# Alignment in a chained attention kernel: a boundary lag of two slots, scans seeded from PSUM, and the teacher rows loaded during the stage before

## The chip, the cores and the metric

One core of a Trainium2 chip runs the whole program in one launch. The metric is the device time of that launch in microseconds (us). A core has five engines that run on their own and meet at semaphores: TensorE (PE in the rows, its weight loads PEld), VectorE (DVE), ScalarE (ACT), GpSimd (POOL) and SyncE (SP), from whose queue most DMAs of this kernel are issued.

## The reference, cut to what matters

The program is a chain of four layers on `x` (8 batches of 256 rows of 256 numbers): cross attention, a mixture of experts that takes one expert a row, an alignment, a gated feed-forward, and further attention and expert layers. The change lies in the alignment and in the expert layer ahead of it. The alignment takes the teacher rows `ctx` (`small` below) and the layer-normalised rows of `x` (`large`) of each batch, finds the cheapest monotone path between them (dynamic time warping), and adds to each row of `x` the teacher rows that the path puts beside it.

```python
def _pairwise_euclidean(a, b):
    aa = jnp.sum(a * a, axis=-1)[:, None]
    bb = jnp.sum(b * b, axis=-1)[None, :]
    ab = a @ b.T
    return jnp.sqrt(jnp.maximum(aa + bb - 2.0 * ab, 0.0))

def _dtw_cost(D):          # R[i, j] = D[i, j] + min(R[i-1, j], R[i, j-1], R[i-1, j-1])
    ...

def _align_one(small, large):
    D = _pairwise_euclidean(small, large)
    R = _dtw_cost(D)
    i_idx, j_idx, valid = _backtrack(R, T_small, T_large)
    contrib = small[i_idx] * valid[:, None].astype(small.dtype)
    expanded = jnp.zeros((T_large, d), dtype=small.dtype).at[j_idx].add(contrib)
    return expanded
```

## The kernel before

`program` (L2775) runs the stages one after the other. Each is a function with its own tiles and semaphores in a `Scope`, closed by a barrier of all engines, and each lists the instructions of every engine by hand, in the order in which that engine takes them. All tensors are float32 where nothing else is said. `P` is 128, `NT` 16 is the number of row tiles, `QT` 2 the row tiles of a batch, `DC` 2 the halves of the 256 features.

**`moe` (L1821), called as `l0f` ahead of the alignment.** After the routing, 23 blocks (`NB`) of 128 gathered rows go through one expert each. GpSimd issues the indirect DMAs (expert weights `fetch`, rows `gather`, results `scatter`), and a block whose expert is that of the block two before fetches no weights. TensorE turns the rows (`turn`, L1895, read by VectorE in `read_t`, L2034, which counts `b_read`), multiplies up (L1911) and down (L1923); ScalarE applies Gelu in `gelu(j)` (L1950, L1957), eight activations a block; VectorE adds the bias. SP has four stores of the rows ahead of the blocks and nothing to issue during them; at the end it waits for all results (L1886) and loads them back. `keep_busy` (L79) issues matmuls on the identity whose result nobody reads.

**`alignment` (L2166), the stage that the change is about,** in four parts.

*Distances.* VectorE computes row statistics in `RowStats`: `moments` (L102) for the first 4 row tiles, then for the other 12, ScalarE takes the roots. GpSimd normalises two tiles a batch into `xn` (L2374), and fills the whole of `d` with 0 after the second batch (L2378) and the whole of `r` with a large number after the fourth (L2380). TensorE turns a batch (L2286), VectorE scales the turned rows by -2 (`minus_two`, L2462), ScalarE squares them (L2396), TensorE makes the products with the turned teacher rows `aT` (L2297) and the column sums of the squares (L2304). ScalarE also squares the teacher rows `ctx` with a sum for each (`aa`, L2420) and copies the column sums (L2403). VectorE adds the three terms into `d2` (`squared`, L2473), ScalarE cuts at zero and takes the root (L2407, L2409), and SP stores the batch to `dist` in DRAM (L2256). `d2` and its store semaphore `dd_out` have two buffers. SP first issues the loads of `aT` for batches 0 and 1, of `ctx` (2 MB), and of `aT` for 2 and 3 (256 KB each); `aT` for batches 4 to 7 follow as buffers come free. After the last store has landed SP loads `dist` back as `d` in a skewed layout (L2261, L2264): partition `8k + b` holds rows `16k` to `16k + 15` of batch `b`, moved right by `LAG * k` columns.

*Recurrence.* A slot `t` handles one column in each of the 16 row blocks (`KB`), block `k` at column `t - LAG * k`. There are `SLOTS = S + LAG * (KB - 1)` of them. VectorE takes the minimum of the two neighbours in the previous column (L2492) and then scans down the 16 rows (`tensor_tensor_scan`, L2497: `state = min(state, near) + d`). The scan starts from the last row of the block above, which another partition made `LAG` slots before: TensorE moves it by eight partitions with the matrix `shift` (L2317), ScalarE adds `outside` (a large number for the first block, 0 for the others) and writes it to `r[:, 0, 2 + t]` (L2430), from where the scan reads its start. Three semaphores carry this: `step` (a scan is done), `moved` (TensorE), `passed` (ScalarE).

```python
for t in range(LAG, SLOTS):                                    # TensorE
    pe.wait_ge(step, t - LAG + 1)
    if t >= LAG + 2:
        pe.wait_ge(passed, t - LAG - 1)
    nc.tensor.matmul(psS[t % 2][:, 0:1], consts["shift"][:], r[:, WB, 2 + t - LAG:3 + t - LAG],
                     start=True, stop=True).then_inc(moved, 1)
```

At slots that are a multiple of `LAG` VectorE also waits for the load of one further block of `d` (`d_first`), and at slot 128 for the right halves (`d_second`).

*Backtrack.* VectorE works through tiles of `CH` x `SLOTS` half-precision elements: comparisons (L2515 to L2518), one long scan (L2519), fifteen rounds of two short operations and a scan (L2523 to L2525), a difference (L2528), fifteen picks of the entries (L2534) and sixteen inside the blocks (L2542). Meanwhile TensorE and ScalarE make keys and values for a later layer (L2330, L2336, L2436 to L2443).

*Spread.* The found spans become 0/1 matrices, and TensorE multiplies them with `ctx` (L2361); VectorE adds to `x`.

## Time and profile before

| | |
|---|---|
| three runs | 2449.93, 2453.03 and 2457.38 us, median 2453.03 |
| the profiled execution | 2449.72 us, its span 2447.9 us |
| granted TensorE clock, mean over the span | 0.828 of full |
| busy share of the span: PE, DVE, ACT, POOL | 81%, 65%, 48%, 39% |

"Busy" is the time in which an engine executes, as a share of the span from the first to the last instruction. The stages follow one another, so a share is an average over stretches that have different limits. All instants below are us from the start of the span. "x16" is the number of instructions in a row; "[3.08 <-DVE ...]" says that the engine sat idle for 3.08 us and which work ended that; SPq and POOLq are the issuing of DMAs. A fp32 matmul stands as two instructions.

### The profile page before, as it was taken

The page shows a single profiled execution, that of the slowest core. Times are in us where ns is not written, and L with a number is a line of the kernel's source. Part 1 is how long each engine was busy: PE and PEld are TensorE (multiplying, and loading weights), DVE is VectorE, ACT ScalarE, POOL GpSimd, SP SyncE. Part 2 cuts the span into 40 slices and gives each one's busy share as a digit, 9 for nine tenths or more (in the row PEclk, how much of TensorE's full clock was granted, in tenths as well). Part 3 has the DMA queues.
Part 4 walks back from the last instruction along what each step waited for, and adds up shares of the span by engine and source line. Part 5 has one row for each costly group of instructions (what it writes and reads, how often), then busy time and mean ns, then how long its engine had stood idle before and what let it go on. Part 6 is the DMA issues. An engine that isn't in the chain of part 4 may idle for free. (4 is left out here: it accounts for less than half of the span.)

```text
span 2447.9 us, 40733 instructions
## 1 busy us (share of the span) xinstructions
PE 1983.4 (81%) x13451; PEld 1615.2 (66%) x13451; DVE 1596.9 (65%) x5265; ACT 1182.9 (48%) x3292; POOL 952.3 (39%) x918
## 2 busy tenths in 40 slices
PE   7985999599948967977999937777777877775788
PEld 5663898499937855655999925566665656654555
DVE  6775111588973247853111168999999999993786
ACT  3544232455321115543232325787777787773354
POOL 3311454300007023303555525666666666661210
PEclk9997999755779989987999975586777778767899
DMA  3112565520314012305364330010000000002442
GB/s 96 62 49 90 195 242 176 150 35 1 120 38 178 0 65 75 104 32 193 128 214 148 103 121 25 1 40 10 31 31 18 31 10 22 31 10 83 154 155 77
DMA packets 102085, 204.56 MB, mean 84 GB/s; under 512 B 20318, under 2 KB 70774, under 8 KB 93942
## 3 DMA queue, kind: packets, MB, share of 16 engines
q1 hardware_dynamic: 77752, 116.23, 14.3%
q0 software_dynamic: 23808, 85.50, 10.2%
q8 instruction: 109, 1.79, 0.3%
q14 instruction: 96, 0.79, 0.1%
q10 hardware_dynamic: 320, 0.26, 0.0%
HBM read 216.31 MB, written 55.35 MB: 111 GB/s over the span
## 5 line engine op out<-in xcount | busy, mean ns | idle before, releaser
L814 DVE MATCH_REPLACE8 l3a_left<-l3a_top,l3a_left 128x256 f32<-128x256 f32 x768 | 309.2, 411 | 0.0
L807 DVE MAX8 l3a_top<-l3a_left 128x8 f32<-128x256 f32 x768 | 286.4, 415 | 0.0
L514 POOL TENSOR_TENSOR l3a_prob<-l3a_expd,l3a_rest 128x512 f32<-128x512 f32 x128 | 162.7, 1271 | 210.3 <-ACT l3a_rest L596 209.4
L369 PEld LDWEIGHTS l3a_psO<-l3a_probT,l3a_vp 128*128 128x128 f32 x1024 | 182.3, 264 | 69.1 <-ACT l3a_probT L612 39.5
L369 PE MATMUL l3a_psO<-l3a_probT,l3a_vp 128*128 128x128 f32 x1024 | 206.3, 365 | 24.1 <-ACT l3a_probT L612 24.1
L351 PE MATMUL l3a_psT<-all_ident,l3a_prob 128*128 128x128 f32 x512 | 111.6, 358 | 108.9 <-POOL l3a_prob L514 108.3
L501 POOL TENSOR_TENSOR l3a_kept<-l3a_raw_sc,l3a_mone 128x512 f32<-128x512 f32 x128 | 163.5, 1277 | 69.4 <-ACT l3a_raw_sc L580 65.8
L1957 ACT ACTIVATE l2f_hT<-l2f_psH,l2f_wt 128x128 f32<-128x128 f32 x312 | 89.2, 369 | 209.5 <-PE l2f_psH L1911 209.5
L507 POOL TENSOR_TENSOR l3a_sc_sb<-l3a_kept,l3a_mlow 128x512 f32<-128x512 f32 x128 | 165.4, 1292 | 10.0
L351 PEld LDWEIGHTS l3a_psT<-all_ident,l3a_prob 128*128 128x128 f32 x512 | 79.6, 184 | 125.7 <-POOL l3a_prob L514 125.4
L2317 PE MATMUL dtw_psS<-dtw_r,all_shift 128*128 128x1 f32 x596 | 152.7, 356 | 10.2 <-DVE dtw_r L2497 9.8
L2317 PEld LDWEIGHTS dtw_psS<-dtw_r,all_shift 128*128 128x128 f32 x596 | 149.2, 311 | 14.0 <-DVE dtw_r L2497 10.8
L1911 PEld LDWEIGHTS l2f_psH<-l2f_xsT,l2f_wt 128*128 128x128 f32 x1248 | 145.3, 192 | 3.4 <-DVE l2f_xsT L2038 1.5
L1911 PE MATMUL l2f_psH<-l2f_xsT,l2f_wt 128*128 128x128 f32 x1248 | 145.8, 275 | 1.0 <-DVE l2f_xsT L2038 1.0
L596 ACT ACTIVATE l3a_rest<-l3a_left,l3a_nmax 128x256 f32<-128x256 f32 x256 | 116.0, 503 | 62.2 <-DVE l3a_left L814 61.8
L1923 PE MATMUL l2f_psY<-l2f_wt,l2f_hT 128*128 128x256 f32 x624 | 141.0, 379 | 0.0
L1923 PEld LDWEIGHTS l2f_psY<-l2f_wt,l2f_hT 128*128 128x128 f32 x624 | 115.6, 190 | 14.2
L2627 POOL TENSOR_TENSOR l1f_kx<-l1f_kx,l1f_cosT 128x512 f32<-128x512 f32 x8 | 11.0, 1374 | 280.2 <-DMA l1f_kx<-k_at 280.2
L589 ACT ACTIVATE l3a_expd<-l3a_sc_sb,l3a_nmax 128x256 f32<-128x256 f32 x256 | 116.3, 501 | 4.1
L1988 POOL DMA_INDIRECT l2f_wt<-in_L_table,l2f_widx x78 | 79.9, 1024 | 97.4 <-ACT l2f_hT L1957 49.3
L2430 ACT ACTIVATE dtw_r<-dtw_psS,all_outside 128x1 f32<-128x1 f32 x298 | 77.9, 261 | 81.4 <-PE dtw_psS L2317 81.4
L1957 ACT ACTIVATE l0f_hT<-l0f_psH,l0f_wt 128x128 f32<-128x128 f32 x184 | 52.7, 368 | 128.8 <-PE l0f_psH L1911 128.8
(571 smaller groups left out, 4725.8 us busy)
## 6 DMA issues: line engine op xcount, KB each, us to landing
key_at<-l3a_a_k SPq DMA_DIRECT2D x8, 768.0 KB, 3.3
kv_at<-dtw_vd SPq DMA_DIRECT2D x8, 512.0 KB, 2.9
k_at<-dtw_kx SPq DMA_DIRECT2D x8, 512.0 KB, 4.3
l1f_kx<-k_at SPq DMA_DIRECT2D x8, 512.0 KB, 4.4
kv_at<-l1f_k SPq DMA_DIRECT2D x8, 512.0 KB, 3.1
l2a_k<-kv_at SPq DMA_DIRECT2D x8, 512.0 KB, 5.7
l2a_vd<-kv_at SPq DMA_DIRECT2D x8, 512.0 KB, 6.7
l2f_yb<-rows_y SPq DMA_DIRECT2D x8, 512.0 KB
```

The costliest lines, as they stand in the source:

```text
L351: mm = nc.tensor.transpose(psT[u % 2][:, kc, e, :], prob[:, u % 4, e, kc * P:kc * P + P], ident[:])
L369: mm = nc.tensor.matmul(psO[y % 2][:, c, 0:P], vp[:, p, kc, c, g * P:g * P + P], probT[:, u % 2, kc, e, :], start=(j == 0 and e == 0 and k ...
L501: nc.gpsimd.tensor_tensor(kept[:], raw_sc[:, u % 2, :, :], mone[:, p, qt, :].unsqueeze(1).to_broadcast([P, 2, S]), ALU.mult)\
L507: nc.gpsimd.tensor_tensor(sc_sb[:, u % 4, :, :], kept[:], mlow[:, p, qt, :].unsqueeze(1).to_broadcast([P, 2, S]), ALU.add)\
L514: nc.gpsimd.tensor_tensor(prob[:, u % 4, :, :], expd[:, u % 2, :, :], rest[:, u % 2, :, :], ALU.subtract).then_inc(picked, 1)
L589: last = nc.scalar.activation(expd[:, u % 2, e, :], sc_sb[:, u % 4, e, :], ACT.Exp, bias=nmax[:, u % 2, e:e + 1])
L807: ins = nc.vector.max(top[:, e, eight], rows[:, e, :] if r else scores[:, e, :])
L814: ins = nc.vector.match_replace(out=rows[:, e, :], in_to_replace=top[:, e, eight], in_values=rows[:, e, :] if r else scores[:, e, :], imm_ ...
L1911: mm = nc.tensor.matmul(psH[2 * p + f // 4][:, f % 4, :], w1[p][c_][f], xsT[:, p, c_, :], start=(c_ == 0), stop=(c_ == DC - 1))
L1923: mm = nc.tensor.matmul(psY[p][:, 0:D], hT[:, p, f, :], w2[p][f], start=(f == 0), stop=(f == FC - 1))
L1957: nc.scalar.activation(hT[:, p, f, :], psH[2 * p + f // 4][:, f % 4, :], ACT.Gelu, bias=wt1[:, p, ROW_B1 + f:ROW_B1 + f + 1]).then_inc(g_d ...
L2317: nc.tensor.matmul(psS[t % 2][:, 0:1], consts["shift"][:], r[:, WB, 2 + t - LAG:3 + t - LAG], start=True, stop=True).then_inc(moved, 1)
```

## The change

- The statistics of the alignment are taken in three groups, of 4, 4 and 8 tiles. VectorE scales batches 0 and 1 before the third.
- A new class `Teacher` holds `ctx_sb`, `aT`, `aa` and their semaphores over both stages. `moe` gets it as `early` (in its first call only): SP loads `ctx` and the first four `aT` after the second transposed read (`b_read` at 2), and ScalarE squares the teacher rows of one batch after the activations of each of blocks 8 to 15.
- `d2` and `dd_out` have four buffers.
- `LAG` is 2, so `SLOTS` is 286 instead of 301, and tiles and passes of that width shrink.
- Two matmuls fill the columns of two PSUM tiles with `outside`. The shift of slot `t` adds to column `t` of one of them. The scan takes its start from that column and covers one row more: row 0, with `near` large and `d` zero, so that it writes its start into `r[:, 0]` itself. ScalarE's step and `passed` go.
- GpSimd fills only the borders of `d`, `near` and `r`, ahead of the normalising.
- TensorE begins the stage with `keep_busy(..., 2)`.

```diff
@@ RowStats
-    def __init__(self, s, nc, x, rstd, mean, negative=False):
+    def __init__(self, s, nc, x, rstd, mean, negative=False, cuts=(FIRST, NT)):
...
     def tiles(self, g):
-        return ((0, self.FIRST), (self.FIRST, NT))[g]
+        return self.cuts[g], self.cuts[g + 1]
@@ moe, sync
+            if early:
+                sp.wait_ge(b_read, 2)
+                early.load(sp)
             for p in range(2):
                 sp.wait_ge(rows_out[p].sem, rows_out[p].base + 16 * ((NB + 1 - p) // 2))
@@ moe, scalar
             for j in range(NB):
                 gelu(j)
+                if early and early.FROM <= j < early.FROM + B:
+                    early.squares(act, j - early.FROM)
@@
+class Teacher:
+    FROM = 8
...
+    def load(self, sp):
+        sp.dma_start(self.ctx_sb[:], self.ctx.rearrange("b (t p) d -> p (b t) d", p=P)).then_inc(self.ctx_in, 16)
+        for b in range(4):
+            self.load_turned(sp, b)
+
+    def squares(self, act, b):
+        if b == 0:
+            act.wait_ge(self.ctx_in, 16)
+        for n in range(b * QT, b * QT + QT):
+            if n >= 2:
+                act.wait_ge(self.aa_done, n - 1)
+            self.nc.scalar.activation(self.junk[:, n % 2, :], self.ctx_sb[:, n, :], ACT.Square,
+                                      accum_out=self.aa[:, n:n + 1]).then_inc(self.aa_done, 1)
@@
-LAG = 3
+LAG = 2
 SLOTS = S + LAG * (KB - 1)
@@ alignment
-        stats = RowStats(s, nc, x, rstd, nmean, negative=True)
+        stats = RowStats(s, nc, x, rstd, nmean, negative=True, cuts=(4, 8, NT))
...
-        d2 = s.sb("d2", [P, 2, QT, S])
-        junk = s.sb("junk", [P, 2, D])
-        d = s.sb("d", [P, WB, SLOTS])
-        near = s.sb("near", [P, 2, WB])
+        d2 = s.sb("d2", [P, 4, QT, S])
+        d = s.sb("d", [P, 1 + WB, SLOTS])
+        near = s.sb("near", [P, 2, 1 + WB])
@@ alignment, sync
-            load(0)
-            load(1)
-            sp.dma_start(ctx_sb[:], ctx.rearrange("b (t p) d -> p (b t) d", p=P)).then_inc(ctx_in, 16)
-            load(2)
-            load(3)
             sp.dma_start(down_at[:], consts["down_at"]).then_inc(tab_in, 16)
             for b in range(B):
                 if b >= 1 and b + 3 < B:
-                    load(b + 3)
+                    sp.wait_ge(d_ps, b)
+                    teacher.load_turned(sp, b + 3)
                 sp.wait_ge(dd_done, b + 1)
@@ alignment, tensor
+            keep_busy(nc, psS[0][:], ident, 2)
             turn(0)
...
                 distances(b)
+            for p in range(2):
+                nc.tensor.matmul(psS[p][:, 0:SLOTS], ident[:], consts["outside"][:].to_broadcast([P, SLOTS]), start=True, stop=False,
+                                 skip_group_check=True)
             for t in range(LAG, SLOTS):
                 pe.wait_ge(step, t - LAG + 1)
-                if t >= LAG + 2:
-                    pe.wait_ge(passed, t - LAG - 1)
-                nc.tensor.matmul(psS[t % 2][:, 0:1], consts["shift"][:], r[:, WB, 2 + t - LAG:3 + t - LAG],
-                                 start=True, stop=True).then_inc(moved, 1)
-            pe.wait_ge(passed, SLOTS - LAG)
+                nc.tensor.matmul(psS[t % 2][:, t:t + 1], consts["shift"][:], r[:, WB, 2 + t - LAG:3 + t - LAG], start=False,
+                                 stop=(t >= SLOTS - 2), skip_group_check=True).then_inc(moved, 1)
@@ alignment, gpsimd
+            nc.gpsimd.memset(d[:, 0:1, :], 0.0)
+            for a, z in ((0, LAG * (KB - 1)), (S, SLOTS)):
+                nc.gpsimd.memset(d[:, 1:, a:z], 0.0).then_inc(pad_set, 1)
+            nc.gpsimd.memset(near[:], BIG).then_inc(corner, 1)
+            nc.gpsimd.memset(r[:, :, 1:2], BIG).then_inc(corner, 1)
+            nc.gpsimd.memset(r[:, 0:1, 2:2 + LAG], BIG).then_inc(corner, 1)
             for b in range(B):
...
-                if b == 1:
-                    nc.gpsimd.memset(d[:], 0.0).then_inc(pad_set, 1)
-                if b == 3:
-                    nc.gpsimd.memset(r[:], BIG).then_inc(corner, 1)
@@ alignment, scalar
-            stats.roots(act)
+            stats.root(act, 0)
+            stats.root(act, 1)
+            act.wait_ge(teacher.aa_done, NT)
             squares(0)
-            act.wait_ge(ctx_in, 16)
+            stats.root(act, 2)
...
-            act.wait_ge(corner, 2)
-            for t in range(LAG, SLOTS):
-                act.wait_ge(moved, t - LAG + 1)
-                nc.scalar.activation(r[:, 0, 2 + t:3 + t], psS[t % 2][:, 0:1], ACT.Identity,
-                                     bias=consts["outside"][:, 0:1], scale=1.0).then_inc(passed, 1)
@@ alignment, vector
                 dve.wait_ge(d_ps, b + 1)
                 dve.wait_ge(b_read, b + 1)
-                dve.wait_ge(aa_done, QT * (b + 1))
-                if b >= 2:
-                    dve.wait_ge(dd_out[b % 2], 16 * (b // 2))
+                if b >= 4:
+                    dve.wait_ge(dd_out[b % 4], 16 * (b // 4))
...
             stats.moments(dve, 0)
             stats.moments(dve, 1)
             minus_two(0)
+            minus_two(1)
+            stats.moments(dve, 2)
             for b in range(B):
-                if b + 1 < B:
+                if 2 <= b + 1 < B:
                     minus_two(b + 1)
                 squared(b)
...
-                nc.vector.tensor_tensor(near[:, t % 2, :], r[:, 1:1 + WB, 1 + t], r[:, 0:WB, 1 + t], ALU.min)\
+                nc.vector.tensor_tensor(near[:, t % 2, 1:], r[:, 1:1 + WB, 1 + t], r[:, 0:WB, 1 + t], ALU.min)\
                     .then_inc(near_set, 1)
                 dve.wait_ge(near_set, t + 1)
                 if t >= LAG:
-                    dve.wait_ge(passed, t - LAG + 1)
-                nc.vector.tensor_tensor_scan(r[:, 1:1 + WB, 2 + t], near[:, t % 2, :], d[:, :, t], r[:, 0, 2 + t:3 + t],
+                    dve.wait_ge(moved, t - LAG + 1)
+                    above_first = psS[t % 2][:, t:t + 1]
+                else:
+                    above_first = r[:, 0, 2 + t:3 + t]
+                nc.vector.tensor_tensor_scan(r[:, 0:1 + WB, 2 + t], near[:, t % 2, :], d[:, :, t], above_first,
                                              ALU.min, ALU.add).then_inc(step, 1)
```

## Rows read from the trace of the kernel before

**Rows 1.** Timeline of the start of the alignment: start us, us busy, instruction, [idle before]
```profile
437.42 0.89 SPq L2243 DMA_DIRECT2D dtw_aT<-in_ctxT  x2
...
439.97 2.17 POOL L2374 TENSOR_SCALAR dtw_xn<-all_x,dtw_nmean,all_rstd 128x256 f32<-128x256 f32 x4 [15.14 <-DVE all_rstd L115]
...
445.23 1.22 DVE L2462 TENSOR_SCALAR dtw_xm<-dtw_psT 128x512 f32<-128x512 f32 x2
...
446.40 3.38 PE L2297 MATMUL dtw_psD<-dtw_xm,dtw_aT 128*128 128x256 f32 x8 [3.08 <-DVE dtw_xm L2462]
...
448.49 0.42 ACT L2420 ACTIVATE dtw_junk<-dtw_ctx 128x256 f32<-128x256 f32 x1 [1.53 <-DMA dtw_ctx<-in_ctx]
```

**Rows 2.** Timeline: distance matmuls of two later batches
```profile
453.95 1.89 PE L2297 MATMUL dtw_psD<-dtw_xm,dtw_aT 128*128 128x256 f32 x8
...
456.98 1.89 PE L2297 MATMUL dtw_psD<-dtw_xm,dtw_aT 128*128 128x256 f32 x8
```

**Rows 3.** A wait (total, times, longest); windows: engines' busy us, PEclk, DMA share, GB/s
```profile
PEld l0f_psY L1923 <- DMA l0f_wt<-in_L_table,l0f_widx: 0.2, 1, 0.2
...
259.00:271.00 12.00, 11.48 (x88) 10.83 (x88) 1.72 (x5) 4.57 (x16) 5.13 (x6) 1.00 0.08 23
...
437.00:449.00 12.00, 4.79 (x14) 3.61 (x15) 8.64 (x39) 3.20 (x8) 8.89 (x10) 0.50 0.86 266
```

**Rows 4.** Timeline of the last batch of distances
```profile
470.97 1.03 PE L2304 MATMUL dtw_psB<-dtw_xsq,all_ones 128*128 128x256 f32 x4
...
473.76 0.88 DVE L2473 SCALAR_TENSOR_TENSOR dtw_d<-dtw_psD,dtw_aa,dtw_bb 128x256 f32<-128x256 f32 x2 [2.14 <-DMA dist<-dtw_d]
...
475.33 0.63 ACT L2409 ACTIVATE dtw_d<-dtw_d 128x512 f32<-128x512 f32 x1
```

**Rows 5.** The recurrence's two lines: ns min/median/max, first and last start us
```profile
L2497 DVE TENSOR_TENSOR_SCAN dtw_r<-dtw_near,dtw_r,dtw_d x301: 251/252/255, 481.5 to 635.5; 128x16 f32<-128x16 f32 x151
...
  ACT dtw_r L2430: 0.7, 3
...
L2492 DVE TENSOR_TENSOR dtw_near<-dtw_r x301: 183/185/189, 481.2 to 635.3; 128x16 f32<-128x16 f32 x151
```

**Rows 6.** Backtrack by lines: busy us, mean ns of one; idle before
```profile
L2525 DVE TENSOR_TENSOR_SCAN dtw_v<-dtw_left,dtw_via 128x301 f16<-128x301 f16 x15 | 11.8, 785 | 0.5
L2519 DVE TENSOR_TENSOR_SCAN dtw_uz<-dtw_left,dtw_uz 128x4832 f16<-128x4832 f16 x1 | 10.2, 10225 | 0.0
...
L2515 DVE TENSOR_TENSOR dtw_dg<-dtw_r 128x4816 f16<-128x4816 f32 x1 | 5.2, 5174 | 0.0
...
L2528 DVE TENSOR_TENSOR dtw_du<-dtw_uz 128x4816 f16<-128x4816 f16 x1 | 2.7, 2673 | 0.0
```

**Rows 7.** Small VectorE operations elsewhere, ns min/median/max
```profile
L2080 DVE TENSOR_TENSOR_SCAN l0f_incl<-l0f_ones,l0f_tot x8: 176/178/191, 232.0 to 232.7; 128x16 f32<-128x16 f32 x8
...
L2549 DVE TENSOR_SCALAR dtw_ends<-dtw_psB x1: 175/175/175, 710.1 to 710.1; 128x16 f32<-128x16 f32 x1
```

**Rows 8.** Timeline of single slots of the recurrence
```profile
482.48 0.25 DVE L2497 TENSOR_TENSOR_SCAN dtw_r<-dtw_near,dtw_r,dtw_d 128x16 f32<-128x16 f32 x1
482.84 0.18 DVE L2492 TENSOR_TENSOR dtw_near<-dtw_r 128x16 f32<-128x16 f32 x1
...
621.81 0.25 DVE L2497 TENSOR_TENSOR_SCAN dtw_r<-dtw_near,dtw_r,dtw_d 128x16 f32<-128x16 f32 x1 [0.24 <-ACT dtw_r L2430]
...
622.12 12.69 PEld L2317 LDWEIGHTS dtw_psS<-dtw_r,all_shift 128*128 128x128 f32 x50 [0.22 <-DVE dtw_r L2497]
...
622.74 0.26 ACT L2430 ACTIVATE dtw_r<-dtw_psS,all_outside 128x1 f32<-128x1 f32 x1 [0.46 <-PE dtw_psS L2317]
```

**Rows 9.** Timeline of the expert stage
```profile
242.69 6.25 PE L83 MATMUL l0f_psX<-all_ident 128*128 128x512 f32 x8
...
259.48 0.42 DVE L2038 COPY l0f_xsT<-l0f_psX 128x256 f32<-128x256 f32 x1 [6.62 <-PE l0f_psX L1900]
...
371.04 1.14 ACT L1957 ACTIVATE l0f_hT<-l0f_psH,l0f_wt 128x128 f32<-128x128 f32 x4 [4.38 <-PE l0f_psH L1911]
```

More of the change, by code:

```diff
@@ L126, in roots @@
     def roots(self, act):
-        for g in range(2):
+        for g in range(len(self.cuts) - 1):
             self.root(act, g)
@@ L2211, in alignment @@
         du = s.sb("du", [P, CH, SLOTS], F16)
-        above_min, side, on = d, (xn, xsq), xm2
+        above_min, side, on = d[:, 1:, :], (xn, xsq), xm2
         psT = [s.ps(f"psT{i}", [P, 512]) for i in range(2)]
@@ L2218, in alignment @@
         ends_ps = psE[:, 0:2 * QT * B].rearrange("p (k q b) -> p k q b", k=2, q=QT)
-        ctx_in, tab_in = s.sem("ctx_in"), s.sem("tab_in")
-        a_in, dd_out = [s.sem(f"a_in{p}") for p in range(4)], [s.sem(f"dd_out{p}") for p in range(2)]
+        tab_in = s.sem("tab_in")
+        a_in, dd_out = teacher.a_in, [s.sem(f"dd_out{p}") for p in range(4)]
         d_first, d_second = [s.sem(f"d_first{k}") for k in range(KB)], s.sem("d_second")
-        x_norm, t_done, m2_done, sq_done, b_ps, b_read, d_ps, d2_done, cut, dd_done, aa_done = (
+        x_norm, t_done, m2_done, sq_done, b_ps, b_read, d_ps, d2_done, cut, dd_done = (
             s.sem(n) for n in ("x_norm", "t_done", "m2_done", "sq_done", "b_ps", "b_read", "d_ps",
-                               "d2_done", "cut", "dd_done", "aa_done"))
-        corner, pad_set, near_set, step, moved, passed = (
-            s.sem(n) for n in ("corner", "pad_set", "near_set", "step", "moved", "passed"))
+                               "d2_done", "cut", "dd_done"))
+        corner, pad_set, near_set, step, moved = (
+            s.sem(n) for n in ("corner", "pad_set", "near_set", "step", "moved"))
         col_set = s.sem("col_set")
```

69 lines of the change are left out of this document (34 added, 35 removed).

## The prediction, made before the changed kernel ran

> **What bounds the kernel now.** I read the page first: its chain that ended last spreads over many stages and names nothing of the alignment, so the change is priced where its code runs, from 437.42 us on in the timeline, and in the expert stage ahead of it. Four stretches matter.
>
> The prologue, 437.4 to 481.2 us, makes the distances [rows 1]. TensorE waits 3.08 us for VectorE, which scales the first tile only at 445.23, after the statistics of all 16 row tiles. The first distance matmuls take 3.38 us, such eight take 1.89 us later [rows 2]: the granted clock is 0.50 (the 1.2 GHz level) to 449 us [rows 3]. From there TensorE goes on with one batch each 3.03 us. At the end VectorE waits 2.14 us for a `dist` store to free one of two buffers [rows 4].
>
> The recurrence, 481.5 to 635.8 us, is VectorE's own two-step chain [rows 5]: 301 slots, each a minimum (185 ns) and a scan (252 ns) with hand-overs of some 35 ns, 0.51 us together. TensorE and ScalarE carry a boundary value for a scan three slots on; it was late only three times, 0.7 us in all. The backtrack, 635.8 to 710 us, is again VectorE back to back [rows 6], with kv work under it. The expert stage is TensorE's: it idled 0.2 us for weights [rows 3].
>
> **Slots.** LAG 2 for 3 makes 256 + 2x15 = 286 slots of 301. From the first scan's start to the last's are 635.5 - 481.5 = 154.0 us over 300 steps, 0.5135 us each, the 16 slots with a further wait for a block of `d` included (their number stays). Fifteen fewer save 7.7 us. The scan gets a 17th element: (785 - 178)/(301 - 16) = 2.1 ns by the scans of 301 and of 16 elements [rows 6, 7], 0.6 us in all. **Saved: 7.1 us** at an unchanged slot.
>
> **Is the shorter lag met?** By the timeline of one slot [rows 8]: the scan starts at 621.81, the shift's weight load at 622.12, ScalarE's read of its result at 622.74. So the result is there 0.93 us after the scan began. The new wait for it stands as a second wait ahead of the next-but-one scan. Where a slot had such a further wait (scan from 482.48 for 0.25 us, next minimum at 482.84), the next instruction started 0.11 us after the scan's end instead of 0.04: 0.07 us more. Together 1.00 us against two slots, 1.02 us. It just fits, since ScalarE's 0.26 us drop out. Behind the wait on VectorE's queue stand that scan and the next minimum, for which TensorE alone is waiting. Bounds: no cost, or a chain 0.06 us longer, half of it per slot: 0.03 x 286 = 8.6 us. I take 0, since each term was seen.
>
> **What a seed in PSUM costs the scan.** No row has a PSUM scalar. The scan of 16 elements from a constant takes 178 ns, this one, from a column in SBUF, 252 ns [rows 5, 7]: the column costs at most 74 ns. Bounds: -74 ns (a PSUM column is free; but then TensorE's chain of 1.00 us holds the slot at 0.50, so in effect -0.01 us a slot, 2.9 us) and +74 ns (it costs twice, 286 x 0.074 = 21.2 us). A tensor read from PSUM is no dearer: 175 ns for a 16-element operation against 185 ns from SBUF [rows 5, 7]. I take 0, by that nearest row.
>
> The Trainium skill, VectorE: DVE Perf Modes, section on the TRN2 errata, charges a VectorE instruction 120 cycles when it reads PSUM and 58 for SBUF; the 62 cycles would be an estimated 65 ns a slot, and the sum would by it end 3.5 us above the time of before. The rows do not show that gap for a tensor input, and no run here shows it for a scalar.
>
> **Prologue.** VectorE's second statistics group shrinks from 12 tiles to 4. Four tiles took from 437.42 to 439.97, with the start; 12 took from there to 445.23 [rows 1]. Four more end near 442.2, where the first scaling now starts. The third group (8 tiles, some 3.9 us between those two) then runs to 447.3 under TensorE's first batch. First distance matmul: 442.9 for 446.40, **3.5 us**. `keep_busy(2)` is four instructions; eight took 6.25 us ahead of the expert blocks [rows 9], so 3.1 us, 437.5 to 440.6, before the first normalised tiles are there at 441.1 (439.97 and half of 2.17): free. It may lift the clock for the first batch, by 0 to 3.38 - 1.89 = 1.5 us; I take 0.7. The first four `aT` tiles are long there and load 4 to 7 come ahead of need by a us or so; nothing counted. Against that ScalarE's third root waits for VectorE until 447 and holds the first copy of the column norms: 0.5 us lost.
> At the end, from the last column sums (472.0) to the last root (475.96) are 3.96 us. With four buffers it is a copy of some 0.4, add 0.88, cut and root 0.63 each and hand-overs, 2.7 us: **1.3 us** [rows 4]. The 5.3 us from root to first minimum stay: store, then first block load; SP has nothing new ahead of them. The seed matmuls come after the last batch, in that time. Sum 3.5 + 0.7 - 0.5 + 1.3 = **5.0 us**, range 3 to 7. Squares of `ctx` leave ScalarE (two of 0.42 us a batch and two accumulator reads, some 1.2 us [rows 1]), under TensorE's 3.03 us, so that counts for nothing. GpSimd's two big fills become six small ones, ahead of 439.97 when it is first needed; uncovered they would cost 1 us once.
>
> **Backtrack.** 286 columns for 301, at each row's slope [rows 6]: three passes of 5.17, one scan of 10.22 and two passes of 2.67 us lose 5% of all but their fixed part, 1.5 us; fifteen rounds lose 32 ns in the scan and 8 ns in each of two operations, 0.7 us; sixteen picks lose 16 ns each, 0.3 us. **2.5 us**, all on VectorE's chain.
>
> **The expert stage**, where things are added. Five loads (3 MB) are issued after the second transposed read, which ends at 259.9 us [rows 9]. From 259 to 271 the queues move 23 GB/s, against 266 from 437 to 449 in the old place [rows 3]. There these loads took from 437.42 to 448.49, 11.1 us [rows 1], so they are in by 271. Cost 0; if the cover is gone, TensorE waits for weights, at the very most those 11.1 us, more likely 2. ScalarE gets those 1.2 us of squares behind the activations of blocks 8 to 15, where it sits idle 4.38 us [rows 9]. Cost 0, and 9.6 us for eight blocks without that cover.
>
> **Sum.** 7.1 + 5.0 + 2.5 = 14.6 us off the profiled execution's own 2449.72 us (span 2447.9 and 1.8 around it): 2435.1 us. The median of the three runs shown is 3.3 us above that execution, so 2438.4 us on its scale. What a measurement of this kernel can tell from no change is 0.3%, 7.4 us.
>
> **Rivals.**
> *TensorE's chain sets the slot.* For it: the margin is 0.02 us. Against: it is made of seen parts, and a longer scan gives it room. A slot of 0.53 us costs 0.02 x 286 = 5.7 us: 2444.1. Chance 0.14.
> *The PSUM seed makes the scan slower*, which ends on the other side. It acts in 286 slots on the engine that bounds them and decides from 14.6/286 = 51 ns on. For it: a column from SBUF already costs up to 74 ns. Against: the tensor reads. At +74 ns: 2438.4 + 21.2 = 2459.6. Chance 0.14.
> *The prologue gives nothing*: the clock and the moved statistics only shift the wait, or the loads meet the weights. 2443.4. Chance 0.10.
> *The half-precision passes lose their double rate.* Rows of 302 elements all began alike, rows of 287 alternate. The two passes would go from 2.67 to about 5 us and thirty short operations gain 0.15 us each: 9.2 us, 2447.6. Against: inputs that begin one element in, and an output in rows of 301, go at that rate now [rows 6]. Chance 0.02. The Trainium skill, same page, Mode 2x_1P, wants 4-byte alignment; by that rule this is what comes, and the trace of before already disagrees.
> *Forecast*: 0.60.
>
> **Numbers.** 2438.4, given as 2438. Below, all bounds at their best (2.0 in the prologue, 2.9 for the slot) and the scatter of some 3 us: 2431. Above, TensorE's chain and the failed prologue together, or three quarters of the PSUM case: 2454. Faster by over 0.3%: the forecast and most of the first and third rival, 0.76. Within 0.3%: the rest of these and a PSUM cost of 25 to 77 ns, 0.17. Slower: more than that, or two mishaps, 0.07.
>
> **What would show it.** The scan's row at 252 to 256 ns if the seed is free, 310 or more if not; scan starts 0.51 us apart, and no waits of the scan for `dtw_psS`. First distance matmul near 442.9 us, first minimum near 476. Passes of 4576 elements near 4.92 and 2.55 us. In the expert stage no wait for `l0f_wt`. A scan or a slot 50 ns longer would make the forecast wrong.

## The result and the profile after

| | before | after |
|---|---|---|
| median of 7 runs each, us | 2454.80 (2449.93 to 2457.38) | 2445.49 (2435.65 to 2451.26) |
| the profiled execution, span, us | 2449.72, 2447.9 | 2445.64, 2443.8 |
| granted TensorE clock, mean | 0.828 | 0.825 |
| busy share: PE, DVE, ACT, POOL | 81%, 65%, 48%, 39% | 81%, 65%, 45%, 39% |

The ratio is 0.996, with an interval of 0.9945 to 0.9975: 0.4% faster, 9.3 us by the medians where 14.6 were forecast. The time lies inside the range given, 7 us above the point.

The whole program is a poor place to read such a change. The alignment alone went from 293.16 to 280.54 us, 12.6 us less, and the stage behind the next three (`l3a`) started 15.1 us earlier (1420.8 for 1435.9), but that execution's two last stages took 10 us longer. So the steps are read from the alignment. All instants with a "+" below are us after the first instruction of an engine that writes a tile of the alignment (437.51 before, 438.17 after).

The start of the alignment after the change, from its timeline (columns as in [rows 1]):

```profile
438.21 3.75 PE L83 MATMUL dtw_psS<-all_ident 128*128 128x512 f32 x4 [14.34 <-PEq L61]
...
440.71 2.17 POOL L2407 TENSOR_SCALAR dtw_xn<-all_x,dtw_nmean,all_rstd 128x256 f32<-128x256 f32 x4 [1.17 <-DVE all_rstd L115]
...
443.02 1.37 DVE L2482 TENSOR_SCALAR dtw_xm<-dtw_psT 128x512 f32<-128x512 f32 x2 [0.17 <-PE dtw_psT L2312]
...
443.86 1.97 PE L2323 MATMUL dtw_psD<-dtw_xm,teacher_aT 128*128 128x256 f32 x8 [0.19 <-DVE dtw_xm L2482]
...
448.83 0.30 PEld L2330 LDWEIGHTS dtw_psB<-dtw_xsq,all_ones 128*128 128x128 f32 x2 [0.38 <-ACT dtw_xsq L2425]
```

The stage starts 0.7 us later than before, so the first distance matmul, at 443.86, stands at +5.68 for +8.90 before [rows 1]. The wait for VectorE is 0.19 us for 3.08, the eight matmuls take 1.97 us for 3.38. The last row is the price of the third statistics group, whose root holds up ScalarE's square: 0.38 us. GpSimd's six small fills are covered: it waits 1.17 us for VectorE before it can normalise. The windows of both stretches (busy us per engine, then granted clock, DMA share, GB/s) answer [rows 3]:

```profile
259.00:271.00 12.00, 11.48 (x86) 10.51 (x85) 1.72 (x5) 4.28 (x16) 4.89 (x5) 1.00 0.84 259
438.00:443.00 5.00, 4.79 (x9) 1.96 (x9) 4.17 (x21) 2.08 (x4) 3.54 (x10) 0.50 0.08 16
443.00:446.30 3.30, 3.11 (x15) 2.62 (x16) 3.28 (x9) 0.60 (x1) 2.17 (x4) 0.98 0.00 0
```

The teacher's loads now fill the queues from 259 us on, where 23 GB/s went before, and TensorE is as busy there as before, 11.48 us of 12. The clock is at its upper level (2.4 GHz) from the first distance matmul on, after 4.8 us of filling and transposes at the lower.

The recurrence and the end of the backtrack's passes, by lines and shapes (busy us, mean ns of one, idle before), answer [rows 5, 6]:

```profile
L2521 DVE TENSOR_TENSOR_SCAN dtw_r<-dtw_near,dtw_psS,dtw_d 128x17 f32<-128x17 f32 x284 | 73.6, 259 | 11.2 <-DVE dtw_near L2513 1.4
L2513 DVE TENSOR_TENSOR dtw_near<-dtw_r 128x16 f32<-128x16 f32 x286 | 54.4, 190 | 17.9 <-DMA dtw_d<-dist 6.8
...
L2521 DVE TENSOR_TENSOR_SCAN dtw_r<-dtw_near,dtw_r,dtw_d 128x17 f32<-128x17 f32 x2 | 0.5, 254 | 0.1
```
```profile
L2549 DVE TENSOR_TENSOR_SCAN dtw_v<-dtw_left,dtw_via 128x286 f16<-128x286 f16 x15 | 11.3, 754 | 0.5
L2543 DVE TENSOR_TENSOR_SCAN dtw_uz<-dtw_left,dtw_uz 128x4592 f16<-128x4592 f16 x1 | 9.7, 9724 | 0.0
...
L2552 DVE TENSOR_TENSOR dtw_du<-dtw_uz 128x4576 f16<-128x4576 f16 x1 | 2.5, 2550 | 0.0
```

The scan takes 259 ns with its start in PSUM and 254 in the first two slots, whose start lies in SBUF; it was 252 with 16 elements. The minimum, whose text was hardly touched, takes 190 for 185. VectorE's waits in the loop name no `dtw_psS`: TensorE's value is always there. The passes are shorter in proportion to 286 of 301 columns, the half-precision ones too.

### The profile page after: what moved, and what is told of

It reads as the page before. It is cut to its first block and busy times, and to the rows that moved or that the text cites. A ratio compares the mean times of both kernels' runs of the same rounds, so it can differ in the third digit from the quotient of the medians.

```text
span 2443.8 us, 40081 instructions
## 1 busy us (share of the span) xinstructions
PE 1991.6 (81%) x13431; PEld 1616.9 (66%) x13431; DVE 1595.4 (65%) x5237; ACT 1105.0 (45%) x2995; POOL 944.3 (39%) x922
## 3 DMA queue, kind: packets, MB, share of 16 engines
q1 hardware_dynamic: 77752, 116.22, 14.5%
## 5 line engine op out<-in xcount | busy, mean ns | idle before, releaser
L2345 PEld LDWEIGHTS dtw_psS<-dtw_r,all_shift 128*128 128x128 f32 x568 | 142.2, 311 | 15.8 <-DVE dtw_r L2521 9.6
L341 PE MATMUL l3a_sc<-l3a_kT,l3a_q 32*128 32x256 f32 x512 | 105.0, 530 | 2.0 <-ACT l3a_q L550 2.0
```

The source lines that it names most:

```text
L2345: nc.tensor.matmul(psS[t % 2][:, t:t + 1], consts["shift"][:], r[:, WB, 2 + t - LAG:3 + t - LAG], start=False, stop=(t >= SLOTS - 2), skip ...
```

## The experiments

This table sets the parts of the alignment side by side, each from one profiled execution (us; the middle columns from the stage's start; "loop" is from the first minimum to the last scan's end). The alignment ends here 0.73 us behind its last instruction, in every row; the expectation of `again` counts to that instruction, 279.8 us for the 280.54 of the table.

| kernel | first distance matmul | last root ends | first minimum | slots, loop | rest | alignment |
|---|---|---|---|---|---|---|
| before | 8.90 | 38.46 | 43.74 | 301, 154.52 | 94.90 | 293.16 |
| after | 5.68 | 32.59 | 37.99 | 286, 150.85 | 91.70 | 280.54 |
| again | 5.41 | 32.31 | 37.69 | 286, 151.07 | 91.34 | 280.09 |
| lag3 | 5.41 | 32.31 | 37.81 | 301, 156.93 | 94.32 | 289.06 |
| old_lag2 | 8.70 | 37.88 | 43.14 | 286, 185.69 | 92.10 | 320.93 |
| wide_r | 5.68 | 32.56 | 38.01 | 286, 150.04 | 91.97 | 280.02 |
| no_early | 5.68 | 37.99 | 43.33 | 286, 150.28 | 90.85 | 284.47 |
| late_sq | 5.67 | 38.82 | 44.10 | 286, 150.43 | 92.14 | 286.66 |
| old_cuts | 8.56 | 37.22 | 42.63 | 286, 150.18 | 91.14 | 283.94 |
| no_busy | 5.67 | 32.99 | 38.28 | 286, 150.89 | 92.57 | 281.74 |
| two_d2 | 5.68 | 33.72 | 38.95 | 286, 150.93 | 91.39 | 281.26 |
| seed_sbuf | 5.68 | 33.05 | 38.35 | 286, 149.56 | 92.17 | 280.08 |
| near_psum | 5.67 | 32.72 | 38.07 | 286, 152.04 | 91.06 | 281.18 |
| best | 5.64 | 32.22 | 37.64 | 286, 154.95 | 91.18 | 283.77 |

Seven of the kernels (`after`, `again`, `lag3`, `wide_r`, `seed_sbuf`, `near_psum`, `best`) have the same prologue: their last root spans 0.8 us and their first minimum 0.7, though up to the fifth batch they agree within 0.3. "Rest" is all but the same code in every row with 286 slots except `old_lag2`, and spans 1.7 us. So the parts are read column by column, where 1 us can be told and 0.3 us cannot, and the sum in the last column is the coarser figure.

### again: the changed kernel once more

No edit. 

> The changed kernel once more, nothing edited. Its alignment stage took 279.8 us in the first profile, 12.6 us less than before, but the two attention stages at the end took 816.2 and 187.8 us against 809.8 and 183.8. Theory A (the late stages' times move from execution to execution, whatever the alignment does): the alignment within 0.5 us of 279.8, the late stages off by several us from 816.2 and 187.8 in either direction. Theory B (the change costs the late stages something): they come out within 1 us of 816.2 and 187.8. The time: about 9 us below before, 0.994 to 0.998.

Measured: 2443.92 us (2435.91 to 2450.84, 7 runs), ratio 0.9948 [0.9927, 0.9969]. The alignment took 280.09 us, the last two stages 806.7 and 188.7 us, where the first profile had 816.2 and 187.8 and the kernel before 809.8 and 183.8. That is theory A: the alignment repeats to half a microsecond and `l3a` alone moves by 10 us between executions of the same code. The 10 us that the last stages seemed to give back were that scatter, and the 12.6 us stand. They would be a ratio of 0.995, which lies inside both intervals. The medians of the whole say 9.3 us in the first comparison and 14.5 in this one (2443.92 against 2458.38 for the kernel before).

### lag3 and old_lag2: what makes a slot

`lag3` puts the three-slot lag back, with seeds in three PSUM tiles; `old_lag2` puts the two-slot lag into the kernel before.

```diff
-LAG = 2
+LAG = 3
+            seeds = [psS[0], psS[1], psB[0]]
-                nc.tensor.matmul(psS[t % 2][:, t:t + 1], ...
+                nc.tensor.matmul(seeds[t % 3][:, t:t + 1], ...
```

> The changed kernel with LAG 3 again: 301 slots, seeds in three PSUM tiles instead of two (the third is one of the column-sum tiles), all else kept. Theory A (a slot's length is VectorE's own two operations; the PE chain has room at LAG 2): scan starts stay 0.52 us apart at the median, the recurrence is 15 slots = 7.9 us longer and the backtrack 2.5 to 3 us, so 10 to 11 us are lost against the changed kernel, and the time is about that of before (ratio 0.998 to 1.002). Theory B (TensorE's chain holds the slot at 0.52): with three slots of room it falls to 0.508 to 0.513, and only 6 to 8 us are lost.

> The kernel before with LAG 2 alone, ScalarE still carrying the boundary. The chain from a scan's start to the seed in SBUF is 0.93 us to ScalarE's start and 0.26 us for its operation, and 0.04 to 0.11 us to the next scan: 1.23 to 1.30 us over two slots. Theory A (the shorter lag needs the seed from PSUM): 0.62 to 0.65 us a slot, recurrence 177 to 186 us for 154, so the kernel loses 20 to 29 us against before in that stretch less 2.5 to 3 in the backtrack: 2468 to 2480 us. Theory B (the lag was free anyway, the seed from PSUM unneeded): slot 0.51, 146 us, the kernel 10 us faster than before.

Measured: `lag3` 2452.99 us (10 runs), ratio 0.9975 [0.9953, 0.9998], alignment 9.0 us longer than `again`. `old_lag2` 2480.11 us (one run), its loop 185.69 us. The lines of the recurrence, first of `lag3`, then of `old_lag2`:

```profile
L2517 DVE TENSOR_TENSOR dtw_near<-dtw_r 128x16 f32<-128x16 f32 x286 | 53.5, 187 | 11.0
L2525 DVE TENSOR_TENSOR_SCAN dtw_r<-dtw_near,dtw_psS,dtw_d 128x17 f32<-128x17 f32 x190 | 49.2, 259 | 7.0 <-DVE dtw_near L2517 0.3
```
```profile
L2497 DVE TENSOR_TENSOR_SCAN dtw_r<-dtw_near,dtw_r,dtw_d 128x16 f32<-128x16 f32 x270 | 68.2, 253 | 45.3 <-ACT dtw_r L2430 35.2 <-DVE dtw_near L2492 0.4
L2492 DVE TENSOR_TENSOR dtw_near<-dtw_r 128x16 f32<-128x16 f32 x271 | 51.4, 190 | 17.2 <-DMA dtw_d<-dist 6.6
```

The scan is 259 ns at either lag, so the shorter lag costs the scan nothing; a slot of `lag3` is 516 ns at the median against 520, and the 4 ns are the minimum's. So TensorE's chain does not hold the slot at a lag of two, theory A in the mechanism. The loss is smaller than A said, the loop 5.9 to 6.1 us longer for 7.9: fifteen slots are 7.7 us, the faster minimum gives back some 1.2 and fewer of the unexplained gaps (last section) some 0.8. The seed in PSUM and the lag belong together: with ScalarE still in the chain VectorE waits 35.2 us for it, and a slot has a mean of 650 ns, theory A's 0.62 to 0.65 us. The seed alone, at the old lag, loses: loop 156.93 for 154.52 us.

### wide_r: the minimum's 5 ns

The minimum took 185 to 187 ns in the two kernels whose rows of `r` lie 303 elements apart, and 190 in those at 288, at either lag. This kernel is the changed one with rows 303 apart.

```diff
-        r = s.sb("r", [P, 1 + WB, 2 + SLOTS])
+        r = s.sb("r", [P, 1 + WB, 17 + SLOTS])
```

> The changed kernel with the rows of r 303 elements apart as before, instead of 288. In the changed kernel the minimum takes 191 ns for 185 and the scan with a PSUM seed 259 ns for 252. Theory A (the distance of r's rows costs it): the minimum is back at 185 ns, the slot at 0.514, 1.5 us saved in 286 slots. Theory B (the minimum's output, which now begins one element in, costs it, or its 17-element neighbour): the minimum stays at 190 or 191 ns, and nothing is saved. The scan: 259 ns by both if its 5 ns are the PSUM seed's.

```profile
L2521 DVE TENSOR_TENSOR_SCAN dtw_r<-dtw_near,dtw_psS,dtw_d 128x17 f32<-128x17 f32 x283 | 73.3, 259 | 11.3 <-DVE dtw_near L2513 1.4
L2513 DVE TENSOR_TENSOR dtw_near<-dtw_r 128x16 f32<-128x16 f32 x284 | 53.1, 187 | 11.1
```

The minimum is back at 186 ns (median), the scan stays at 259, the slot's median is 517, and the loop 0.8 to 1.0 us shorter. The row distance is the cause; only these two distances were tried, and why 288 is dearer than 303 no run here tells. In time: 2443.28 us (10 runs), ratio 0.9937 [0.9918, 0.9955], not told apart from `again`.

### seed_sbuf and near_psum: the price of PSUM

`seed_sbuf` leaves the boundary values between the row blocks out of the recurrence; `near_psum` computes the same as the changed kernel.

```diff
-                    above_first = psS[t % 2][:, t:t + 1]
+                    above_first = consts["outside"][:, 0:1]
```
```diff
+            nearp = psT[0][:, 0:2 * (1 + WB)].rearrange("p (k j) -> p k j", k=2)
-                nc.vector.tensor_tensor(near[:, t % 2, 1:], ...
+                nc.vector.tensor_tensor(nearp[:, t % 2, 1:], ...
-                nc.vector.tensor_tensor_scan(r[:, 0:1 + WB, 2 + t], near[:, t % 2, :], ...
+                nc.vector.tensor_tensor_scan(r[:, 0:1 + WB, 2 + t], nearp[:, t % 2, :], ...
```

> The scan takes its first value from a constant column in SBUF instead of the column in PSUM; the shift matmul, its wait and everything else stay. So the boundary values between the sixteen column blocks are left out of the recurrence. Theory A (reading the scalar from PSUM costs the scan 5 ns and nothing else): scan 254 ns for 259, slot median 515 for 520 ns, loop 1.4 us shorter, 149.5 us. Theory B (the 5 ns belong to the second wait or to the 17th column, not to where the scalar lies): scan stays at 259 ns, slot 520. Theory C (PSUM also delays the next instruction's start, which the scan's own duration does not show): slot 510 or less with the scan at 254.

> The minimum of each slot is written to PSUM and the scan reads its 17 elements from there, on top of the seed; the rest is the changed kernel (and TensorE's kv work waits for the last slot). It doubles the suspected cost of PSUM in a slot and puts it on the tensor operand and on a write. Theory A (PSUM costs a few ns an access at this size, as with the seed): scan 259 to 270 ns, minimum 191 to 200 ns, slot median 520 to 540. Theory B (a fixed price of some 60 ns falls on each access of PSUM, and the seed escaped it as a scalar): scan or minimum 50 to 70 ns longer, slot 575 or more, the loop 16 to 35 us longer.

The recurrence by lines, first of `seed_sbuf`, then of `near_psum`:

```profile
L2521 DVE TENSOR_TENSOR_SCAN dtw_r<-dtw_near,all_outside,dtw_d 128x17 f32<-128x17 f32 x272 | 69.2, 255 | 10.5 <-DVE dtw_near L2513 1.0
L2513 DVE TENSOR_TENSOR dtw_near<-dtw_r 128x16 f32<-128x16 f32 x275 | 52.4, 190 | 17.3 <-DMA dtw_d<-dist 6.7
```
```profile
L2524 DVE TENSOR_TENSOR_SCAN dtw_r<-dtw_psT,dtw_psS,dtw_d 128x17 f32<-128x17 f32 x273 | 70.3, 258 | 10.2 <-DVE dtw_psT L2516 0.6
L2516 DVE TENSOR_TENSOR dtw_psT<-dtw_r 128x16 f32<-128x16 f32 x273 | 54.0, 198 | 10.6
```

With the scalar in SBUF the scan is 254 ns and the slot's median 515 for 520: theory A, 5 ns a slot and nothing hidden behind it, 1.4 us in all. With 17 elements more read from PSUM the scan is not longer at all (258 for 259), and the minimum, which now writes there, takes 7 ns more; the slot's median is 526, theory A again. Both times of the whole (2444.43 and 2448.20 us, one run each) say nothing beyond that.

The Trainium skill, VectorE: DVE Perf Modes, section on the TRN2 errata, whose 62 cycles came to an estimated 65 ns, is contradicted for this kernel: the seed read from PSUM costs 5 ns and a tensor read none. The Trainium skill's 4-byte rule, same page, Mode 2x_1P, is contradicted by the row of `dtw_du` above, 2550 ns for 4576 elements out of rows 287 long, 0.56 ns each where the passes that read float32 took 1.07 before [rows 6].

### no_early, late_sq and old_cuts: what moved the prologue

`no_early` takes the teacher's loads and squares back into the alignment; `late_sq` is that with the squares one place later on ScalarE; `old_cuts` is the changed kernel with statistics of 4 and 12 tiles.

```diff
@@ no_early: moe gets no teacher; alignment, sync and scalar
+            teacher.load_turned(sp, 0)
+            teacher.load_turned(sp, 1)
+            sp.dma_start(ctx_sb[:], ...).then_inc(teacher.ctx_in, 16)
...
-            act.wait_ge(teacher.aa_done, NT)
+                    teacher.squares(act, b)
                     row_norms(b)
@@ late_sq: behind squares(b + 1)
-                    teacher.squares(act, b)
                     row_norms(b)
                 if b + 1 < B:
                     squares(b + 1)
+                if b < B:
+                    teacher.squares(act, b)
@@ old_cuts
-        stats = RowStats(..., negative=True, cuts=(4, 8, NT))
+        stats = RowStats(..., negative=True, cuts=(4, NT))
```

> The teacher's rows and their squares go back into the alignment: five loads issued at its start, two squares per batch on ScalarE between the column norms, VectorE's sum waiting for them; all the rest is the changed kernel. In the changed kernel the first distance matmul starts 5.68 us after the alignment's start, and the last root ends at +32.6 us. Theory A (my prediction's: the moved loads gave nothing, because the first block of aT is there long before it is used and ScalarE's squares lie under TensorE's batch): first distance matmul and last root within 0.5 us of that, alignment 280 to 281 us; the expert stage's last activations end 1 us or less earlier. Theory B: the first block of aT would land only at some +7 us (before, it was wanted only at +8.9), so that the earlier statistics are worth nothing without the earlier loads: first distance matmul at +7 or later, alignment 1.5 to 4 us longer. Theory C: ScalarE's squares between the roots lengthen each batch: first matmul unchanged, last root 1 us or more later.

> The statistics go back to two groups, of 4 and 12 tiles; the loads stay early, the clock is still kept up, the rest is the changed kernel. The first distance matmul then starts after all 16 tiles' statistics: before, that was at +8.9 us with the first scaling at +7.8; now +5.68. Theory A (the third group is what moved the start): first distance matmul at +8.4 to +9.0, alignment 2.5 to 3.3 us longer, 283 us. Theory B (the late third group costs later what the early start gains: ScalarE's root of it sits ahead of the first column norms and VectorE's scaling of later tiles waits): the end of the last root moves by less than 1.5 us, alignment 281 to 282 us.

> As the run with the teacher's rows loaded and squared inside the alignment, but each batch's two squares stand on ScalarE behind the squares of the next batch's transposed tile instead of ahead of the column norms. That run had its first distance matmul at +5.68, its third at +15.24 (changed kernel: +12.06), and its last root at +38.0 us (+32.6), with TensorE waiting 3.5 us for the squared tile, which stood behind ScalarE's wait for the teacher's rows (landed at +12.1). Theory A (it is the place on ScalarE's queue that cost, not the ScalarE time nor the load's): TensorE's wait goes, the third batch's matmuls start at +13 to +14 (held now only by VectorE's sum, which needs the row norms at +13), last root at +34 to +36. Theory B (ScalarE's extra 1.2 us per batch is what cost): last root at +37 or later.

Measured, one run each: 2453.34, 2443.70 and 2453.81 us; the alignment 3.9 to 4.4, 3.4 to 3.9 and 6.1 to 6.6 us longer than in the two runs of the changed kernel. In `no_early` the first distance matmul starts at +5.68 as expected by A (its `aT` is there), and yet the last root ends 5.4 us later. Its timeline:

```profile
454.30 0.42 ACT L2193 ACTIVATE teacher_junk<-teacher_ctx 128x256 f32<-128x256 f32 x1 [2.25 <-DMA teacher_ctx<-in_ctx]
...
455.38 0.58 ACT L2430 ACTIVATE dtw_xsq<-dtw_psT 128x512 f32<-128x512 f32 x1
...
456.01 1.13 PE L2335 MATMUL dtw_psB<-dtw_xsq,all_ones 128*128 128x256 f32 x4 [3.14 <-ACT dtw_xsq L2430]
...
457.44 3.56 PE L2328 MATMUL dtw_psD<-dtw_xm,teacher_aT 128*128 128x256 f32 x8
```

ScalarE stands at the first teacher square until `ctx` has landed, at +12.1, and behind it stands the square that TensorE needs: TensorE waits 3.14 us, and the clock it had is gone, so the third batch's eight matmuls take 3.56 us instead of 1.89:

```profile
447.80:452.00 4.20, 4.12 (x21) 3.68 (x22) 4.05 (x18) 0.85 (x2) 1.56 (x3) 1.00 1.08 358
456.00:461.10 5.10, 5.08 (x18) 4.22 (x19) 2.51 (x6) 3.58 (x12) 1.09 (x2) 0.67 0.18 56
```

The granted clock is 1.00 before the wait and 0.67 after it. Together 3.14 and 1.67 us are 4.8 of the 5.4. That number is theory C's, but its cause is not: from the start of the fourth batch's distance matmuls to the eighth's it is 12.4 us for 12.0 in the changed kernel, and the difference is a wait of 0.44 us for the sixth batch's `aT`. So the squares themselves lengthen no later batch. In the kernel before the same load of `ctx` was in at +10.98 [rows 1], and TensorE's late start covered it. `late_sq` was to take only the queue's part away, and A of its text failed: TensorE's second batch is no longer held and the third starts at +14.15 for +15.24, but the squares now hold VectorE's sum, and VectorE's next scaling, which TensorE needs, stands behind that. VectorE waited for the squares in all eight batches, 16.8 us, and TensorE stood just the same:

```profile
455.73 2.65 PE L2328 MATMUL dtw_psD<-dtw_xm,teacher_aT 128*128 128x256 f32 x8 [1.89 <-DVE dtw_xm L2488]
...
458.18 1.91 PE L2335 MATMUL dtw_psB<-dtw_xsq,all_ones 128*128 128x256 f32 x4
```

So it is the late landing of `ctx` that costs, and the place on the queue chooses who waits. The last root at +38.8 is theory B's number, but B's cause, ScalarE's added 1.2 us a batch, cost nothing a batch in `no_early`. In `late_sq` the new place costs more later on: its last root comes 6.4 us behind the start of the last batch's matmuls, for 5.5 in the changed kernel.

`old_cuts` starts its first distance matmul at +8.56 and is never caught up: first minimum 4.6 to 4.9 us later than in the changed kernel. Theory A has the cause and the start right (+8.4 to +9.0) and the loss too small: behind that start the first eight matmuls take 3.44 us for 1.97, and the sixth batch waits 0.55 us for its `aT`. The two parts are one. Against the kernel before, the early loads without the new cuts gain 1.1 us (42.63 for 43.74, about the buffers' share below), the new cuts without the early loads 0.4 us (43.33), both 5.75 to 6.05; all three figures have the four buffers in them.

### no_busy and two_d2

`no_busy` leaves out the `keep_busy` at the start; `two_d2` goes back to two distance buffers.

```diff
@@ no_busy
-            keep_busy(nc, psS[0][:], ident, 2)
@@ two_d2 (and every index % 4 of d2 and dd_out to % 2)
-        d2 = s.sb("d2", [P, 4, QT, S])
+        d2 = s.sb("d2", [P, 2, QT, S])
```

> The four filling matmuls ahead of the alignment's first transposes are left out. In the changed kernel the granted clock is 0.98 in the first batch and its eight distance matmuls take 1.97 us; before, at 0.50, they took 3.38. Theory A (the filling alone keeps the clock up; worth the 1.4 us measured in the matmuls and up to 1 us more in transposes and column sums): granted clock 0.50 for the first batch, eight matmuls 3.0 to 3.5 us, the last root 1.5 to 2.5 us later, alignment 282 us. Theory B (the clock is up because the work now comes sooner, without the filling): clock near 1, no difference. Theory C: the clock falls, but the first batch waits for other engines anyway: matmuls 3.4 us, alignment within 0.7 us.

> Two distance buffers in place of four; the rest is the changed kernel. Before, VectorE waited 2.14 us for a store in the last batch. Theory A (the prediction's 1.3 us): the wait comes back in the last batches only, the last root ends 1.0 to 2.2 us later, alignment 281.1 to 282.5 us. Theory B (with an earlier start, all batches run sooner than the stores return, so that every batch waits): 3 us or more longer. Theory C (the four buffers gave nothing, the stores are in time): within 0.5 us.

Measured, one run each: 2450.54 and 2446.11 us. Without the filling the first eight distance matmuls take 2.63 us for 1.97, and the fifth batch's start at +18.53, for +18.04 to +18.27 in the seven kernels with the same prologue: 0.3 to 0.5 us. The last root, 0.4 to 0.7 us later than in the changed kernel's two runs, is inside those kernels' own spread. That is theory C's size in the prologue, with less of a fall in the clock than C named; the rest of the alignment's 1.2 to 1.7 us stands in the column that scatters. From `old_cuts` comes the condition of its use:

```profile
446.94 3.44 PE L2323 MATMUL dtw_psD<-dtw_xm,teacher_aT 128*128 128x256 f32 x8 [3.15 <-DVE dtw_xm L2481]
```

There the filling ran just as long, then TensorE waited 3.15 us, and the first batch took 3.44 us at a granted clock of 0.57 all the same. In these runs the filling lifted the clock only for work that followed it at once.

With two buffers VectorE's waits come back, in six batches and not in the last ones alone:

```profile
DVE dtw_d L2492 <- DMA dist<-dtw_d: 10.8, 6, 2.6
```

10.8 us of waiting, of which 1.0 to 1.3 us reach the first minimum: theory A in the sum, B in the rows. TensorE's batch of 3.03 us hid the rest. The kernel before had five such waits, 9.1 us in all, of which the prediction read the last.

### best: an attempt at more

```diff
-        ... d_first = [s.sem(f"d_first{k}") for k in range(KB)]
+        ... d_first = [s.sem(f"d_first{k}") for k in range(5)]
-                    .then_inc(d_first[k], 16)
+                    .then_inc(d_first[k.bit_length()], 16)
-                if t % LAG == 0 and t // LAG < KB:
-                    dve.wait_ge(d_first[t // LAG], 16)
+                if t in (0, LAG, 2 * LAG, 4 * LAG, 8 * LAG):
+                    g = (t // LAG).bit_length()
+                    dve.wait_ge(d_first[g], 16 * max(1, 2 ** (g - 1)))
```

> The changed kernel with the rows of r 303 elements apart in place of 288, and with five waits for blocks of d in place of sixteen: the blocks count up on five semaphores (block 0, 1, 2 to 3, 4 to 7, 8 to 15), waited for in slots 0, 2, 4, 8 and 16. The slots with a further wait were 70 ns longer than the rest, fifteen of them. Expected: eleven of these gone, 0.8 us; with the 5 ns of the minimum (0.9 us) and some 0.3 us in the rest of the alignment 1.7 to 2 us less than the changed kernel, alignment 278.5 to 279.5 us, ratio to the kernel before 0.994. Rival: the grouped blocks land later than their slot and the scan waits for them at slots 4, 8 or 16: loop as long as with sixteen waits or longer.

Measured: 2446.45 us (7 runs), ratio 0.9954 [0.9936, 0.9971]; the loop 154.95 us, 3.9 to 4.1 us longer than in the changed kernel. The rival came true; VectorE's timeline:

```profile
481.18 0.19 DVE L2514 TENSOR_TENSOR dtw_near<-dtw_r 128x16 f32<-128x16 f32 x1 [0.85 <-DMA dtw_d<-dist]
...
485.12 0.19 DVE L2514 TENSOR_TENSOR dtw_near<-dtw_r 128x16 f32<-128x16 f32 x1 [1.90 <-DMA dtw_d<-dist]
...
492.97 0.19 DVE L2514 TENSOR_TENSOR dtw_near<-dtw_r 128x16 f32<-128x16 f32 x1 [3.76 <-DMA dtw_d<-dist]
```

These three instants are the landings of blocks 3, 7 and 15: (492.97 - 485.12)/8 = 0.98 us a block. I had counted on half of that, the pace at which SP issues the loads (14 in 6.46 us in the changed kernel). That mean hides the pace: in this run SP issues the first twelve 0.36 us apart, and from the fourteenth on they are 0.9 to 1.2 us apart. With sixteen waits and a lag of two, a block is wanted every 2 x 0.52 + 0.07 = 1.11 us. The sixteen waits are worth their 70 ns each against this grouping, others were not tried, and the first thirty slots now run within some 12% of their loads. No kernel here beats the changed one by a difference that the runs can tell.

## Why the prediction was right, and where not

The forecast (0.60) was the case that came, and its sum of 14.6 us stands against 12.6 measured in the alignment. That it is only 2 us off is in part luck: the slots gave 3.4 us less than forecast, prologue and backtrack together 1.5 more.

- **Slots: 7.1 us forecast, 3.7 measured** (154.52 to 150.85). This is the term that was mis-sized. The seventeenth element costs the 2 ns it was given. Taking 0 for the seed in PSUM was wrong by 5 ns, 1.4 us, well inside the bounds of -74 and 74. That the minimum would stay at 185 ns was not even a step of the sum; it rose by 5 ns with the row distance of `r`, 1.4 us more. The last 0.6 us are four slots with a gap some 0.25 to 0.32 us too long, where before there were three of 0.21. The signs named for the scan (252 to 256 ns) and for the scan starts (0.51 us apart) were missed by a little, 259 ns and 0.52 us.
- **"It just fits"** was right: VectorE waits for `dtw_psS` in no run, and there are 35 ns between minimum and scan as before. The fit is wider than the 0.02 us of the prediction. The 0.07 us for a second wait don't belong in that chain, since the scan stood behind two waits before the change too, at the same gap; that leaves 0.93 against 1.04 us. And the three waits for ScalarE, 0.7 us [rows 5], were misread: each time the value was written 0.54 us before the scan started (at 621.81 in [rows 8], for one), so these were gaps of the kind told in the last section. The rival of TensorE's chain is refuted. The rival of the seed, which needed 51 ns to decide, is refuted by 5.
- **Prologue: 5.0 forecast, 5.75 measured** (first minimum at +37.99 for +43.74). Start 3.2 for 3.5; clock 1.4 in the matmuls for 0.7, though leaving the filling out takes back 0.66 of it in the matmuls and 0.3 to 0.5 at the fifth batch, so half or less of it is the filling's; third root 0.38 for 0.5; buffers 1.0 to 1.3 for 1.3. Of the `aT` loads 4 to 7, which were to come a us ahead of need, one did not: TensorE waited 0.34 us for the sixth batch's in the kernel before and 0.48 in `seed_sbuf`, whose prologue is the changed kernel's, though not in `after`.
- **The step that failed though the sum held**: that moving the squares of `ctx` "counts for nothing". I asked whether ScalarE's 1.2 us a batch fit under TensorE's 3.03, and they do, as the later batches of `no_early` show. I did not ask when `ctx` lands, though the row was there: +10.98, with a ScalarE wait of 1.53 us [rows 1]. With the start moved up by some 3 us that landing would have become the limit, and `no_early` shows it: without the moved loads 5.3 of the prologue's 5.75 us are lost. The forecast of the prologue held because the change moved the loads too, not because the prediction knew that they were needed. The rival that the prologue gives nothing named the new clock, the statistics and the loads meeting the weights, not this.
- **Backtrack: 2.5 forecast**, 2.2 measured up to the first matmul that spreads the teacher's rows (77.13 to 74.92), and 3.2 with the rest, where kernels of the same code differ by up to 1.7.
- **Expert stage: 0 forecast**, 200.5 us for 200.1, and 259 GB/s where there were 23. The cover named there (ScalarE's idle time at 371 us) still holds 3.58 us of 4.38.
- **The half-precision rival** is refuted: 2550 ns against 2673 for the same pass.
- **A sum was wrong**: the one from the Trainium skill's figures for PSUM (VectorE: DVE Perf Modes, the TRN2 errata) was given as 3.5 us above the time of before; 286 times the estimated 65 ns are 18.6 us, less 14.6 it is 4.0.

## What to carry to other kernels

Before an engine's start is moved up, list everything that arrives by its own clock (a load, another engine's result) and compare its instant with the new need, not with the old: what was covered by the late start is the next limit, and the two parts of such a change can be worth next to nothing singly and 4.5 to 5 us together (the 5.75 to 6.05 less the buffers' share). A recurrence of half a microsecond a step is priced in nanoseconds, each taken 286 times, and a row distance belongs to that price as much as the operation. Where single stages scatter by 10 us between executions, read the changed stage in the trace and let the whole program's ratio only bear it out.

## What the runs showed of the hardware that was not expected

- VectorE's minimum over 16 rows took 190 ns with the rows 288 float32 apart and 186 with 303, everything else equal (`wide_r`); so also in `lag3` (303: 187) and `old_lag2` (288: 190). Other distances were not tried.
- A column in PSUM as the scan's start cost 5 ns more than one in SBUF; 17 elements read from PSUM cost nothing more, writing 16 cost 7 ns.
- A pause of 3.1 us took TensorE's granted clock from 1.00 to a mean of 0.67 over the next 5 us, so that the pause cost half as much again in the work behind it (`no_early`), and 3.75 us of filling were lost when a pause of 3.15 us followed (`old_cuts`).
- Some slots have a gap between minimum and scan for which no wait accounts, as in this row of the changed kernel's loop:

```profile
621.04 0.26 DVE L2521 TENSOR_TENSOR_SCAN dtw_r<-dtw_near,dtw_psS,dtw_d 128x17 f32<-128x17 f32 x1 [0.36 <-DVE dtw_near L2513]
```

They fall on the same slots (20, 61, 146, 274, counted from 0) in `after`, `again`, `wide_r` and `seed_sbuf`, in `no_busy` and `two_d2` too, and on others in the remaining kernels, so they go by the place in the program and not by the data. 61 and 146 are 85 slots apart. The kernel before has three, in slots 60, 145 and 273, which its profile puts down to ScalarE, whose value was there. What happens in them no run here settles.
